# A long-convolution layer with a feed-forward block on one core: near lags ahead of state and readout, work by chunk pairs, a last tile by blocks

## The reference

```python
xp = (jnp.einsum('btd,de->bte', X, Wp) + bp).reshape(B, T, STAGES + 1, D)
pos = sine_positional_encoding(T, D, X.dtype)
f = (pos @ Wf + bf).reshape(T, STAGES, D)
...                       # xp and f padded with zeros to 2T
F = jnp.fft.rfft(f, axis=0)
y = xp[:, :, 0, :]
for i in range(STAGES):
    conv = jnp.fft.irfft(jnp.fft.rfft(y, axis=1) * F[None, :, i, :], n=L, axis=1)
    y = conv * xp[:, :, i + 1, :]
...
x = _layernorm(x + y)
gate = jnp.einsum('bsd,hd->bsh', x, wg)
up = jnp.einsum('bsd,hd->bsh', x, wu)
x = _layernorm(x + jnp.einsum('bsh,dh->bsd', jax.nn.silu(gate) * up, wd))
```

## Time and profile before

| | |
|---|---|
| Median of three runs | 809.74 us |
| Profiled execution | 810.85 us, span 808.9 us |
| PE busy | 765.6 us (95%) |
| DVE, ACT, POOL busy | 556.9, 490.7, 434.4 us |
| Chain that ended last | PE 84%, DVE 6%, issue 3%, POOL 3% |
| Filter load, 1024 KB, to landing | 7.5 us (median) |
| POOL `hl` subtraction, 128x512 | 1157 ns (mean of 96) |

### The profile page before, as it was taken

One profiled execution on the slowest core, in us unless ns is written; L12 is line 12 of the kernel. 1 busy time (PEld: TensorE's weight loads), 2 busy tenths in 40 slices (PEclk: granted clock), 3 DMA queues, 4 the chain that ended last, 5 costly groups with the idle time before them and its releaser, 6 DMA issues.

```text
span 808.9 us, 16504 instructions
## 1 busy us (share of the span) xinstructions
PE 765.6 (95%) x6068; PEld 573.3 (71%) x6068; DVE 556.9 (69%) x1173; ACT 490.7 (61%) x977; POOL 434.4 (54%) x564
## 2 busy tenths in 40 slices
PE   5999989999799999999999999789999999999993
PEld 4888868888588888888888877546655665566652
DVE  4777777777688888888887887645665565656551
ACT  3455554444377777777776664366577756776652
POOL 3445535445144444444444445687778778777452
PEclk9999999999899999999999999899999999999997
DMA  8659757998998888888889894311111221111001
GB/s 276 206 188 314 258 185 264 327 311 288 279 252 251 248 248 243 237 238 251 249 245 282 249 287 161 92 53 48 57 53 53 79 78 53 53 59 47 27 27 53
DMA packets 161151, 144.99 MB, mean 179 GB/s; under 512 B 4016, under 2 KB 144304, under 8 KB 160816
## 3 DMA queue, kind: packets, MB, share of 16 engines
q1 hardware_dynamic: 159232, 138.49, 56.6%
q10 hardware_dynamic: 1840, 5.44, 2.0%
HBM read 109.58 MB, written 34.34 MB: 178 GB/s over the span
## 4 chain that ended last, share of the span: by engine, by line
PE 84%; DVE 6%; issue 3%; POOL 3%; DMA 2%; ACT 1%; SPq 0%; DVEq 0%; ACTq 0%; POOLq 0%
PE bank L356 21%; PE bank L426 19%; PE bank L408 17%; PE bank L447 11%; PE bank L369 6%; DVE prod L745 3%; PE bank L390 3%; PE bank L392 2%; PE bank L391 2%; DVE yl L776 2%; PE bank L418 2%; POOL x L227 1%; DMA toep<-filter_rows 1%; DMA toep<-in_WP 1%; PE bank L468 1%
## 5 line engine op out<-in xcount | busy, mean ns | idle before, releaser
L908 POOL TENSOR_TENSOR y<-y,gate 128x256 f32<-128x256 f32 x192 | 139.2, 728 | 183.2 <-DVE y L768 171.2
L408 PE MATMUL bank<-prod,ei 128*128 128x256 f32 x720 | 201.4, 403 | 0.0
L356 PE MATMUL bank<-wps,xs 128*128 128x512 f32 x768 | 183.2, 398 | 10.6 <-DVE wps L703 8.3
L356 PEld LDWEIGHTS bank<-wps,xs 128*128 128x128 f32 x768 | 145.2, 191 | 42.6 <-issue 8.3
L935 POOL TENSOR_TENSOR xs<-xt,xs 128x256 fp32r<-128x256 f32 x128 | 93.2, 743 | 107.0 <-ACT xs L539 106.9
L426 PE MATMUL bank<-xh,wq 128*128 128x512 f16 x384 | 145.6, 379 | 2.7 <-DVE hf L808 1.5
L426 PE MATMUL bank<-xl,wq 128*128 128x512 f16 x384 | 145.5, 379 | 0.0
L927 POOL TENSOR_TENSOR hl<-hf,hh 128x512 f16<-128x512 f32 x96 | 110.2, 1157 | 53.6 <-ACT hh L596 53.5
L408 PEld LDWEIGHTS bank<-prod,ei 128*128 128x128 f32 x720 | 125.0, 193 | 10.5
L768 DVE SCALAR_TENSOR_TENSOR y<-bank,iscl,y 128x256 f32<-128x256 f32 x180 | 87.1, 484 | 64.4 <-PE bank L408 63.3
L808 DVE SCALAR_TENSOR_TENSOR hf<-bank,sg 128x512 f32<-128x512 f32 x96 | 64.2, 684 | 92.3 <-ACT sg L592 47.4
(11 more groups left out here) (65 smaller groups left out, 1247.7 us busy)
## 6 DMA issues: line engine op xcount, KB each, us to landing
toep<-filter_rows SPq DMA_DIRECT2D x43, 1024.0 KB, 7.5
gates<-toep SPq DMA_DIRECT2D x48, 512.0 KB, 4.0
gate<-gates SPq DMA_DIRECT2D x48, 512.0 KB, 4.3
xt<-in_XT SPq DMA_DIRECT2D x32, 512.0 KB, 5.2
xr<-in_X SPq DMA_DIRECT2D x16, 512.0 KB, 4.9
out_x<-oo SPq DMA_DIRECT2D x16, 512.0 KB, 3.3
toep<-filter_rows SPq DMA_DIRECT2D x10, 512.0 KB, 6.6
ei<-in_EI ACTq DMA_DIRECT2D x2, 1024.0 KB, 6.4
```

The lines of the kernel that those rows point to most:

```text
L356: mm = pe.matmul(b_proj[n % PBK][:, :], xs[:, n % XSS, hx, k, :], wps[:, hw, k, p * 512:(p + 1) * 512], start=(k == 0 and q == 0), stop=(k ...
L408: mm = pe.matmul(b_out[n % 2][:, 0:W], ei[:, h, e0 * P:(e0 + 1) * P], prod[:, n % 3, h, :], start=(h == 0), stop=(h == 1))
L908: nc.gpsimd.tensor_tensor(y[:, u % NG, a, :], y[:, u % NG, a, :], gate[:, a, :], ALU.mult).then_inc(gated, 1)
```

## The change

On PE a step of the unit loop is now `toeplitz`, `state`, `readout`; before it was `state`, `toeplitz`, `readout`. The transposes of the first tile go one step sooner. `readout` fills the two halves of a PSUM bank with two chunks, and `gather` and `apply` take two chunks in one instruction (eight and nine a unit instead of 15 and 16); the squares and the gate loads that follow come up to two steps later. The staging buffer has half its space in memory of its own (`st0`), so that the first filter of slot 1 is loaded while the second projection pass still runs. Four weight buffers instead of two. The first layer norm's steps are moved in the last unit. The last tile's down product runs by blocks of the hidden width (`down_last`), its last low half is made by DVE instead of POOL, and its norm and store go by halves. The first input and the first weights are loaded in parts.

```diff
+NPAIR = NA // 2
+NGATE = NPAIR + 1
...
-            wi = sb("wi", [P, 2, HID], I32, ffn)
+            wi = sb("wi", [P, 4, HID], I32, ffn)
...
-        spare = sb("spare", [P, 512])
+        st0 = sb("st0", [P, 2, NG, W])
...
+
+                for b in range(NB):
+                    sp.dma_start(xt[:, 0, :, b], XT[:, :, 0, b]).then_inc(x0_in[b], 16)
+                sp.wait_ge(wp_in[0], 16)
+                sp.wait_ge(wp_in[1], 16)
                 load_x(1)
...
+                    if p == 1 and a == 13:
+                        load_filter(NSUB + 1)
                     sp.wait_ge(proj_used, NB * (m + 1))
...
+                            sp.dma_start(gate_ap[2 * s, a], st[m % 2][:, s].rearrange("p g w -> p (g w)")).then_inc(g_out[m % 2], 16)
                 sp.wait_ge(g_out[1], NA // 2 * 16 + 7 * 32)
                 load_gate(0, 0)
-                load_filter(NSUB + 1)
                 load_gate(0, 1)
-                load_gate(0, 2)
                 sp.wait_ge(g_out[1], NA // 2 * 48)
                 load_filter(NSUB + 2)
+                sp.wait_ge(g_out[0], NA // 2 * 48)
+                load_gate(0, 2)
                 load_gate(0, 3)
                 for u in range(NU):
                     if u == NU - 2:
...
-                        load_weights(1)
+                        for e in range(4):
+                            load_weights(e)
                         load_rows(1)
                         sp.dma_start(ident[:], IDENT).then_inc(id_in, 16)
                     for j in range(4):
...
                             else:
-                                sp.wait_ge(gated, u * NA + 4 * j + 4)
+                                sp.wait_ge(gated, u * NGATE + 2 * j + 3)
...
+                def down_last(k):
+                    pe.wait_ge(zz_ready, k * 2 + 1)
+                    for m in range(HM):
+                        pe.wait_ge(hh_ready, k * HM + m + 1)
+                        if m < HM - 1:
+                            pe.wait_ge(hl_ready, k * HM + m + 1)
+                        else:
+                            pe.wait_ge(hl_last, 1)
+                        for b in range(NB):
+                            for h in (hh, hl):
+                                mm = pe.matmul(b_d[b // 2][:, (b % 2) * D:(b % 2 + 1) * D],
+                                               h[:, k % 2, m, b * P:(b + 1) * P], wd[:, m, :],
+                                               start=(m == 0 and h is hh and b % 2 == 0),
+                                               stop=(m == HM - 1 and h is hl), skip_group_check=True)
+                            if m == HM - 1 and b % 2:
+                                mm.then_inc(d_done, 1)
 
...
-                        if u < NU and k < NE:
-                            state(u, k)
                         if k == 0 and 1 <= u < NU:
                             toeplitz(u, NQ - 1, 1)
...
-                        if k == 11 and u == NU - 1:
+                        if k == 10 and u == NU - 1:
...
+                        if u < NU and k < NE:
+                            state(u, k)
+                        if k >= 2 and u < NU:
+                            readout(u, k - 1)
                         if k == 14 and u == NU - 1:
                             pe.wait_ge(w_cast, 6)
                             pe.wait_ge(norm_sum, NU)
                             gate_part(0, 0)
-                        if k >= 2 and u < NU:
-                            readout(u, k - 1)
...
-                act.dma_start(wp[:, :, 0:512], WP[:, :, 0:512]).then_inc(wp_in, 16)
+                act.dma_start(wp[:, 0, 0:512], WP[:, 0, 0:512]).then_inc(wp_in[0], 16)
+                act.dma_start(wp[:, 1, 0:512], WP[:, 1, 0:512]).then_inc(wp_in[1], 16)
...
-                        if k % 2 == 0 and k >= 6 and u < NU - NG:
-                            square(u, k // 2 - 3)
-                        if k in (0, 2, 4) and 0 <= u - 1 < NU - NG:
-                            square(u - 1, 5 + k // 2)
+                        if k % 2 == 0 and k >= 8 and u < NU - NG:
+                            square(u, k // 2 - 4)
+                        if k in (0, 2, 4, 6) and 0 <= u - 1 < NU - NG:
+                            square(u - 1, 4 + k // 2)
...
-                def gather(u, a):
-                    n = u * NE + a - 1
-                    if a == 1:
+                def gather(u, j):
+                    m = u * NPAIR + j
+                    a, count = 1 + 2 * j, 2 if j < NPAIR - 1 else 1
+                    if j == 0:
                         dve.wait_ge(toep_out, NQ * (u + 1))
-                    dve.wait_ge(r_done, n + 1)
+                    dve.wait_ge(r_done, u * NE + a - 1 + count)
                     nc.vector.scalar_tensor_tensor(
-                        out=y[:, u % NG, a, :], in0=b_out[n % 2][:, 0:W], scalar=unscale(u),
-                        in1=y[:, u % NG, a, :], op0=ALU.mult, op1=ALU.add).then_inc(z_done, 1)
+                        out=y[:, u % NG, a:a + count, :],
+                        in0=b_out[m % 2][:, 0:count * W].rearrange("p (a w) -> p a w", w=W), scalar=unscale(u),
+                        in1=y[:, u % NG, a:a + count, :], op0=ALU.mult, op1=ALU.add).then_inc(z_done, 1)
 
...
-                            gather(u - 1, NA - 2 + k)
-                        if k >= 3 and u < NU:
-                            gather(u, k - 2)
+                            gather(u - 1, NPAIR - 2 + k)
+                        if k >= 5 and k % 2 and u < NU:
+                            gather(u, (k - 5) // 2)
                         if u < NU and k < NE:
                             multiply(u, k)
                         if k % 2 == 0 and u + 1 < NU:
                             low(u + 1, k // 2)
...
-                            if k in (6, 9):
-                                stats1((k - 6) // 3, (k - 6) // 3 + 1)
-                            if k == 13:
+                            if k in (5, 10):
+                                stats1(k // 5 - 1, k // 5)
+                            if k == 12:
                                 low_x(0)
                 for k in range(NA):
...
-                sum2(NA - 1)
-                stats2(NA - 1, 2 * NA)
+                k = NA - 1
+                dve.wait_ge(hh_ready, k * HM + HM)
+                nc.vector.tensor_tensor(hl[:, k % 2, HM - 1, :], hf[:, (HM - 1) % 3, :], hh[:, k % 2, HM - 1, :],
+                                        ALU.subtract).then_inc(hl_last, 1)
+                stats2(k - 1, count2(k))
+                dve.wait_ge(oo_ready, k * NB + 1)
+                for h in range(2):
+                    sum2_half(k, h)
+                    dve.wait_ge(zz_ready, k * 2 + h + 2)
+                    for b in (2 * h, 2 * h + 1):
+                        last = nc.vector.bn_stats(bst[:, 1, b, :], zz[:, b, :])
+                    last.then_inc(stats, 1)
...
+                def apply(u, j):
+                    a, count = (0, 1) if j == 0 else (2 * j - 1, 2 if j < NPAIR else 1)
+                    if j == 0:
                         pool.wait_ge(toep_out, NQ * (u + 1))
                     else:
-                        pool.wait_ge(z_done, u * NE + a)
-                    if a % 4 == 0:
-                        pool.wait_ge(gate_in[a // 4], (u + 1) * 16)
-                    nc.gpsimd.tensor_tensor(y[:, u % NG, a, :], y[:, u % NG, a, :], gate[:, a, :],
-                                            ALU.mult).then_inc(gated, 1)
+                        pool.wait_ge(z_done, u * NPAIR + j)
+                    if j % 2 == 0 and j < NPAIR:
+                        pool.wait_ge(gate_in[j // 2], (u + 1) * 16)
+                    nc.gpsimd.tensor_tensor(y[:, u % NG, a:a + count, :], y[:, u % NG, a:a + count, :],
+                                            gate[:, a:a + count, :], ALU.mult).then_inc(gated, 1)
 
...
-                first_applied = ([], [], [], [0], [1], [2], [3, 4], [5], [6], [7, 8]) + tuple([k - 1] for k in range(10, NA))
                 for u in range(NU + 1):
                     for k in range(NA):
-                        if k == 0 and u >= 1:
-                            apply(u - 1, NA - 1)
-                        for a in first_applied[k] if u == 0 else [k - 1]:
-                            if u < NU and a >= 0:
-                                apply(u, a)
-                        if u == NU - 1 and k in (4, 7):
-                            pool.wait_ge(gated, u * NA + (k - 4) // 3 + 1)
-                            add((k - 4) // 3)
-                        if u == NU - 1 and k in (8, 11):
-                            root(0, (k - 8) // 3 + 1)
+                        if k <= 1 and u >= 1:
+                            apply(u - 1, NPAIR - 1 + k)
+                        if k == 2 and u < NU:
+                            apply(u, 0)
+                        if k >= 5 and k % 2 and u < NU:
+                            apply(u, (k - 3) // 2)
+                        if u == NU - 1 and k in (2, 7):
```

(18 more changed lines are left out.)

119 lines of the change are left out of this document (71 added, 48 removed).

## The result

| | before | after |
|---|---|---|
| Median of four runs beside each other | 810.19 us | 840.65 us |
| Lowest and highest | 809.26, 812.15 | 839.26, 841.73 |
| Profiled execution (span) | 810.85 (808.9) us | 839.26 (837.5) us |
| PE busy | 95% | 90% |

After over before is 1.0377, with a 95% interval of 1.0364 to 1.0390. The forecast was 845 us, range 836 to 855.

What follows compares the result with a forecast made beforehand. PE's own work was taken to bound the kernel. Terms 48.8 - 6.6 + 0.3 - 2.7 - 3.6 - 0.7 = +35.5 on the profiled 810.85 gave 846.4, or 845 us from the median; range 836 to 855.

Steps and rivals of the forecast that it cites:

- The new wait: Unit loop: PE stands still 0.72 us for DVE's low half at odd steps, some 88 times; a pair costs 3.82 us.
- the loop term: Eleven units of the loop at 30.3 us instead of 25.87: +48.8 us.
- The clock: Unit loop: granted clock taken as 1.00; rival, it goes down in the short stops, about 955 us, chance 0.03.
- Gather and gating by pairs: DVE in the unit loop: wide gather 0.75 us, hidden; saves about 1.5 us of DVE a unit, none of the time.
- Filters: Early filter load removes the 4.16 us stop and half clock, -6.6; rival, filters 1 us late each, about 889, chance 0.03.
- Last unit: Last unit: 23.0 us instead of 24.8, -1.8, and about 1 more before the first down product: -2.7 us.
- Last tile: End of the kernel: down product starts at once by blocks, norm and store by halves: -3.6 us, bounds -6 to -1.5.
- The longer estimate: Last tile by the skill's port rule: up to one POOL subtraction, 1.16 us, lost; the term -2.4 instead of -3.6.
- First loads: Start of the kernel: half the weights come sooner for PE's first matmul, between 0 and -1.5: -0.7 us.
- the +0.3 at the projections: Projections: the early filter load may hold one store up for up to 1 us: +0.3, bounds 0 to 1.5.
- The low half is in time: Rival, unit loop: no wait, the loop gains 0.08 at each of 14 readouts a unit, 12.3 us: 784 us, chance 0.05.

Runs made afterwards that it cites:

- e9: e5 with ACT's squares two steps sooner, at the steps where the kernel before has them: 779.57 us, ratio 0.9622.
- e6: The kernel before with only the first input loaded in four parts and the first weights in two: 809.16 us, ratio 0.9976.
- e3: The changed kernel with PE's order state, readout, near lags: 782.68 us, ratio 0.9653.
- e5: e3 with DVE's wide gather moved to the even steps, ahead of multiply: 779.12 us, ratio 0.9620.
- e8: The changed kernel with PE's old order and the first filter of slot 1 loaded behind the first gate again: 799.82 us, ratio 0.9856.
- e4: The changed kernel in its own PE order, with DVE's low half ahead of the even step's multiply: 783.62 us, ratio 0.9666.
- e11: The kernel before with only PE's order changed to state, readout, near lags: 795.07 us, ratio 0.9815.
- e7: The kernel before with only the last tile's down product by blocks, last low half on DVE, norm and store by halves: 806.71 us, ratio 0.9939.

## Why the prediction was right, point by point

**The new wait.** Right in place, cause and size. The forecast was some 88 waits of 0.72 us and a pair of 3.82; measured are 88, 0.73 us in the pair shown, and pairs of 3.8. PE's wait for multiply ahead of the next state, forecast as met in time, shows at about one step a unit. Readout at 0.86, multiply to `low` at 0.61 (271.07 to 271.68) and near lags 0.10 behind the end of `low` are all as taken from the earlier trace rows. The unit came out 30.19 instead of 30.3, so the loop term is +47.5 instead of +48.8.

**The clock.** Right. PE was idle 16% of every pair and the granted clock stayed at 1.00, the level of 2.4 GHz, in both stretches above and over the whole loop (203 to 536 us). (The half-clock step of that rival adds up to 3.24 us, not 3.15; nothing hangs on it.) The rule of the Trainium skill that was weighed here (TensorE: Matmul & The Clock Gate, "A second HAM failure mode: psum-queue depth-cycling"), that frequent short pauses send the clock to and fro, is not borne out by stops of 0.5 to 0.9 us every 3.8 us. Longer single stops are another matter: the half clock of before begins within a stop of 4.16 us (up to 217.45), within one of 3.17 us (from 506.86) and just behind one of 3.65 us (up to 791.93), and that of e9 just behind one of 1.74 us, while the same stops of 3.2 and 3.7 us in e6 left the clock at 1.00. So such a stop may bring the half clock or not.

**Gather and gating by pairs.** Hidden, as forecast: the wide gather took 0.74, estimated at 0.75, and stands where DVE was idle. Only in the faster orders does its place matter: about 3.6 us between e3 and e5.

**Filters.** The stop went, -6.4 against -6.6, and e8 gives -5.0 to -5.9. No filter was late at a unit of 30.19. The rival had the right place and the wrong time. It takes a unit near 25 us and the late squares together: e3, e4 and e5 have such waits, e9 and e11, with units of 24.65 and the squares at their old steps, have none in their steady units. In e5 PE's own waits come to 3.0 us in all, not 1 us a load.

**Last unit, mis-sized: -4.9 instead of -2.7.** The working of the part after was close: multiply 0 at 534.95, multiply 14 at 557.61, so 22.66 us against a forecast of 23.0. The row of before was misread. Multiply 0 is not at 499.55 but two multiplies earlier:

```profile
496.64 0.68 DVE L745 TENSOR_TENSOR prod<-bank,wfx 128x512 f32<-128x512 f32 x1
...
498.27 0.68 DVE L745 TENSOR_TENSOR prod<-bank,wfx 128x512 f32<-128x512 f32 x1
```

So before took 27.68 us, not 24.8, and the first part of the term is -5.0 instead of -1.8. Whoever counts operations of one form in a trace must count from an event that occurs once. The second part, about -1 for the run-up to the first down product with its four weight buffers, isn't there: from multiply 14 it takes 21.54 us before and 21.63 after. What of the -5.0 belongs to the edit is open. PE's longest stop in this unit fell from 3.17 us to 1.60, and the half clock of 6.83 us is gone; but e6 and e7, whose last unit is that of before, take 29.3 and 29.4 us for the same 14 steps with only 3.41 us at half the clock.

**Last tile: -4.8 between the two traces, -3.6 forecast.** Some 1.6 us of the 4.8 are the half clock at 792.28 in the trace of before, which the forecast had also read its rows from; against e6, which lacks it, the term is -3.2 (e7 by medians -4.7, with 3.3 to 6.6 as interval). So the size was about right. Up to the free `zz` the steps agree: from the end of `hh` (823.06) to 829.41 is 6.35, forecast 6.4. What follows is shorter. The root of a half is 0.70 for 128x2 where 128x4 takes 1.01 (at 825.96 in this trace), and from the last normalise to the end it is 2.66 us (834.84 to 837.5) instead of the 3.4 of a whole tile. By the rule of the Trainium skill (SBUF — State Buffer, the reading of its port diagram) DVE's subtraction at 823.09 should have waited for POOL's instruction, which had started first. POOL's L999 ran from 822.03 to 823.19 and took its usual 1.16, DVE's took 0.69, as in all nine traces that have it. The two overlap by only 0.10 us, so this case shows that nothing was lost and not whether the rule holds. The longer estimate that went with it was not needed.

**First loads, mis-sized: -2.75 instead of -0.7, and nearly half of it is luck.** PE's first row after, and three stretches of the first projections, two of before and one of after:

```profile
6.76 9.94 PE L373 MATMUL bank<-wps,xs 128*128 128x512 f32 x36 [6.76 <-DVE wps L748]
```

```profile
9.00:13.50 4.50, 4.50 (x12) 3.55 (x11) 1.11 (x2) 0.42 (x1) 2.48 (x4) 1.00 0.97 363
14.10:18.60 4.50, 4.50 (x21) 3.68 (x20) 3.45 (x8) 2.33 (x5) 2.20 (x3) 1.00 1.06 333
```

```profile
9.80:14.30 4.50, 4.50 (x21) 3.68 (x21) 3.53 (x7) 2.21 (x4) 2.94 (x5) 1.00 1.01 379
```

The first matmul is 1.55 sooner than in the earlier trace rows, a little past the bound. (Over all traces it starts at 8.1 to 8.3 us with the old loads and at 6.5 to 7.8 with the split ones.) The other 1.2 us lie in the first 36 matmuls, which take 9.79 us instead of 10.98. They start 0.43 us apart and later 0.23, about the two levels of the clock; the trace has no entry of the clock before that moment, where the view prints 1.00. The quick pace begins at about 14.0 us before, behind 13 slow matmuls, and at about 9.8 after, behind seven: six times 0.20 us is 1.2. The split doesn't bring this about. e7, with the old loads, has eight to nine slow ones and 10.05 us for the 36, and e6, with the split loads, eleven and 10.55. So the loads are worth the earlier start, 1.55 us in this pair, and the forecast missed that part by 0.85.

**The sum.** The three terms at the edges were short by 5.5 us in all, loop and filter together forecast 1.1 too slow, and the +0.3 at the projections didn't show. So the change of the span came out 6.9 us below the forecast (28.6 against 35.5). The medians differ less, by 4.4 (840.65 against 845), since the profiled execution of before stood 1.1 us above its median and that of after 1.4 below its own; that part is luck. So is some 2.8 us of what the edges were short, the clock of one execution at the start and in the last tile. None of this touches the sign, which rests on one wait.

**The rivals.** "The low half is in time" was wrong for this kernel, and its price of 784 us was right: e4 makes its condition true and takes 783.62 (27.0 us under its own runs of before, where the rival had 25.6).

## What to carry to other kernels

When an order on one engine is changed, write down for each wait of the moved block what the releasing engine has to do in between, and how much of the waiter's own work used to cover it. Here 1.28 us of multiply and `low` were covered by near lags, readout and state, and afterwards by the readout alone. The remedy is often on the other engine: an instruction whose inputs are early should not stand behind one whose input is late.

## What the runs showed of the hardware

- With PE idle for 0.5 to 0.9 us in every 3.8 us, over 333 us, the granted clock stayed at 1.00 (84% busy).
- The clock makes up to 1.6 us between executions of the same code in one stretch: six to 14 slow matmuls at the start, and a last down product at 0.50 or at 1.00 behind equal stops of 3.65 and 3.66 us (before and e6).
- The two fp32 products of a readout take 0.86 to 0.87 us from their start to the next block when they stand behind the 256-column fp16 matmuls of `state`, and 0.94 behind the 64-column ones of the near lags. Over the loop that 0.08 is most of the 1.9% of e11.
- A gather of 128x512 takes 0.74 us on DVE against 0.48 for 128x256. The gating product on POOL gains less from width: 1.28 against 0.73.
- A DMA share of 0.94 to 0.95 at 260 GB/s (e5 and e9, 230 to 430 us) left PE busy 98% of the time, as this row of e9 shows. A share that high isn't by itself a sign that transfers hold PE up.

```profile
230.00:430.00 200.00, 196.37 (x2429) 167.04 (x2428) 171.67 (x289) 160.55 (x314) 85.12 (x75) 1.00 0.95 261
```
